# Input rows standardised on ScalarE with a scale and a bias, VectorE left with the bias column

## The reference, cut to what matters

```
def _layernorm(x, axis=-1, eps=1e-05):
    m = jnp.mean(x, axis=axis, keepdims=True)
    v = jnp.var(x, axis=axis, keepdims=True)
    return (x - m) / jnp.sqrt(v + eps)
...
    h = _layernorm(x, axis=-1) * (1 + ca) + sa
    x = x + ga * _L0_attn_ref(h, ...)       # q, k, v, gates; recurrent state; layernorm; silu gate; Wout
    h = _layernorm(x, axis=-1) * (1 + cb) + sb
    x = x + gb * _L0_ffn_ref(h, ...)        # router, top 2 of 8 experts, gelu
```

## Time and profile before

| | |
|---|---|
| median of 3 runs | 1010.74 us (1009.75 to 1011.5) |
| the profiled execution, its time | 1011.38 us |
| its span, first to last instruction | 1009.6 us |
| PE busy over the span | 902.7 us (89%) |
| DVE busy | 733.6 us (73%) |
| ACT busy | 479.1 us (47%) |
| POOL busy | 427.0 us (42%) |
| mean granted TensorE clock | 0.968 of full speed |

### The profile page before, as it was taken

One profiled execution on the slowest core, in us unless ns is written; L12 is line 12 of the kernel. 1 busy time (PEld: TensorE's weight loads), 2 busy tenths in 40 slices (PEclk: granted clock), 3 DMA queues, 4 the chain that ended last, 5 costly groups with the idle time before them and its releaser, 6 DMA issues.

```text
span 1009.6 us, 27138 instructions
## 1 busy us (share of the span) xinstructions
PE 902.7 (89%) x7313; PEld 743.9 (74%) x7314; DVE 733.6 (73%) x1909; ACT 479.1 (47%) x1548; POOL 427.0 (42%) x452
## 2 busy tenths in 40 slices
PE   4989999999999999997189999999999989999895
PEld 4556655656655656654179998999999989999895
DVE  2469999999999999997646666666566666666663
ACT  1556566666566665563034434343434433434432
POOL 5335665555655555653213333333323323233233
PEclk9789999999999999998579999999999999999998
DMA  7901111111111111111282222222222222222221
GB/s 240 375 27 52 54 45 51 53 39 52 53 42 53 53 38 53 53 38 39 83 278 40 39 37 37 38 43 32 43 32 43 39 36 38 37 38 38 39 39 24
DMA packets 51451, 62.68 MB, mean 62 GB/s; under 512 B 6273, under 2 KB 46930, under 8 KB 51282
## 3 DMA queue, kind: packets, MB, share of 16 engines
q1 hardware_dynamic: 38546, 44.36, 13.9%
q0 software_dynamic: 12864, 17.83, 10.3%
HBM read 38.91 MB, written 23.27 MB: 62 GB/s over the span
## 4 chain that ended last, share of the span: by engine, by line
PE 61%; DVE 14%; issue 9%; DVEq 6%; ACT 3%; SPq 3%; DMA 3%; POOL 0%; ACTq 0%; POOLq 0%
PE p_a L1084 19%; PE p_cum L1084 8%; PE p_z L1084 8%; PE p_qk L1084 8%; PE p_vg L1084 7%; PE p_o L1084 6%; DVE w_hi L842 4%; SPq L444 2%; PE p_tr L1084 1%; PE p_tr L1266 1%; DMA host_x<-in_L_attn_x_dram 1%; DVE x L917 1%; PE p_o L1103 1%; DVE host_s_r L1068 1%; DVEq L1033 1%
## 5 line engine op out<-in xcount | busy, mean ns | idle before, releaser
L641 POOL DMA_INDIRECT out_dram<-x,tok x68 | 163.6, 2405 | 344.3 <-DVE x L1061 318.7
L661 ACT ACTIVATE h2T<-p_tr,mods 128x128 f32<-128x128 f32 x200 | 80.6, 453 | 345.0 <-PE p_tr L1266 290.3
L1084 PE MATMUL p_a<-w_hi_r,host_s_r 128*128 x544 | 145.2, 299 | 11.8 <-DVE host_s_r L1068 11.8
L1084 PE MATMUL p_a<-w_r,host_s_r 128*128 x544 | 139.8, 289 | 0.0
L590 POOL TENSOR_TENSOR w<-qkT_both,own_half 128x512 f32<-128x512 f32 x64 | 65.0, 1035 | 165.4 <-ACT qkT_both L735 155.8
L1038 DVE COPY host_x<-w 128x1024 f32 x68 | 47.3, 696 | 98.0 <-issue 52.0
L1084 PEld LDWEIGHTS p_a<-w_hi_r,host_s_r 128*128 128x128 f32 x544 | 101.8, 187 | 14.2 <-issue 13.9
L1084 PEld LDWEIGHTS p_a<-w_r,host_s_r 128*128 128x128 f32 x544 | 101.9, 187 | 0.3
L842 DVE TENSOR_TENSOR w_hi<-p_a,upto 128x512 f32<-128x512 f32 x128 | 84.3, 679 | 4.1 <-PE p_a L1084 4.1
L621 POOL DMA_INDIRECT expert_rows<-rows,pos x64 | 63.9, 999 | 51.7 <-POOL rows L618 22.5
L1084 PE MATMUL p_qk<-h2T,host_x 128*128 128x128 f32 x544 | 68.8, 281 | 7.0 <-DVE qkT_both L1038 5.9
(11 more groups left out here) (208 smaller groups left out, 2085.4 us busy)
## 6 DMA issues: line engine op xcount, KB each, us to landing
w<-in_L_ffn_W_dram SPq DMA_DIRECT2D x16, 1024.0 KB, 12.5
ln_host<-expert_rows SPq DMA_DIRECT2D x68, 136.0 KB, 2.1
host_x<-in_L_attn_x_dram SPq DMA_DIRECT2D x64, 128.0 KB, 2.1
out_dram<-x SPq DMA_DIRECT2D x32, 128.0 KB, 1.7
w<-in_L_wmod_dram SPq DMA_DIRECT2D x1, 1536.0 KB, 6.4
expert_rows<-pad_rows SPq DMA_DIRECT2D x8, 136.0 KB, 1.8
out_dram<-x,tok POOLq DMA_INDIRECT x68, 4.7
b_all<-in_L_ffn_b_dram SPq DMA_DIRECT2D x1, 1024.0 KB, 7.5
```

What stands on the lines that cost most here:

```text
L641: nc.gpsimd.indirect_dma_start(out=out, out_offset=bass.IndirectOffsetOnAxis(ap=tok[u][:, 0:1], axis=0), in_=y_out[u][:], in_offset=None, ...
L661: last = A.activation(dst[:, j, :], src[:, j * P:(j + 1) * P], ACT.Identity, scale=mods[:, which + 2 + j:which + 3 + j], bias=mods[:, whic ...
L1084: return nc.tensor.matmul(dst, lhsT, rhs, start=start, stop=stop, skip_group_check=True)
```

## The change

DVE no longer writes the standardised rows. It waits for `x_scale` as before and makes one column, -mean * scale, in column 3 of `mv_x`, in one instruction of 128x1. ACT then writes `xn` as scale * x + bias in one `Identity` activation of 128x256, whose scale and bias are both columns of `mv_x`. A new semaphore `x_shift` goes from DVE to ACT. ACT does this between the gate's Ln (L714) and the copy of the output (L718). `xn_ready` now comes from ACT, and the wait for `xT_ready` of the chunk before, which guards `xn`, moves to ACT with it. For chunk 0 ACT does it right behind the inverse root.

```diff
+        x_shift = sem("x_shift")
...
+            def standardise_x(c, slot):
+
+                act_e.wait_ge(x_shift, c + 1)
+                after(act_e, xT_ready, c - 1)
+                A.activation(xn[slot][:], x_in[slot][:], ACT.Identity,
+                             scale=mv_x[:, 2:3], bias=mv_x[:, 3:4]).then_inc(xn_ready, 1)
+
             def modulate_x(c):
...
             inverse_root(mv_x, 0, x_stats, x_scale)
+            standardise_x(0, 0)
             act_e.wait_ge(mods_taken, 1)
...
                     A.activation(lg[:], eg[:], ACT.Ln, bias=1.0).then_inc(gate_log1p_ready, 1)
+                if nextx:
+                    standardise_x(s + 2, u)
                 if finish:
                     act_e.wait_ge(owT_ready, s)
...
             def norm_x_end(n, u):
-                after(dve, xT_ready, n - 1)
-                standardise(xn[u][:], x_in[u][:], mv_x, n, x_scale).then_inc(xn_ready, 1)
+                dve.wait_ge(x_scale, n + 1)
+                V.tensor_scalar(mv_x[:, 3:4], mv_x[:, 0:1], mv_x[:, 2:3], -1.0, ALU.mult, ALU.mult).then_inc(x_shift, 1)
```

## The result

The changed kernel takes 1025.35 us (median of 4 runs, 1024.51 to 1026.56), the kernel before 1011.12 us beside it: 14.2 us or 1.4% slower, ratio 1.014, 95% interval 1.0127 to 1.0153. Predicted were 1024.4 us, 13.7 more.

What follows compares the result with a forecast made beforehand. Bound: a dependence ring through PE, ACT and DVE, with ACT's and DVE's branches tied at L904. 13.5 us (steps 3 to 29) plus 0.2 (step 2) made 13.7, on 1010.74: 1024.4 us, range 1017 to 1028.

Steps and rivals of the forecast that it cites:

- The two tied branches: From L868, DVE's and ACT's parallel work meet at the forget gate L904; ACT's branch claimed as long, with nothing to spare.
- The ring: Loop of dependences x1, PE, ACT, DVE and back to x1; a delay of x1 goes round once every step.
- the other meeting on the ring: DVE's L942, claimed to be released by ACT's L748, starting 0.05 us after that ends.
- The price of the activation: Time the new Identity holds ACT between L714 and L718: 0.50 us per step, lower bound 0.31 to 0.33 us, upper 626 ns.
- 27 x 0.50: Cost over steps 3 to 29, which have the tight meeting at L904: 13.5 us.
- two estimates, 0.46 and 0.54: Two ways to price the activation's hold on ACT, in us: from L661, and from L714 plus the columns' cost.
- VectorE's relief: DVE ready 0.16 to 0.24 us earlier at `mask(2)`, taken as 0.2; worth nothing unless ACT's branch shortens too.
- the limit that the prediction had seen at 306.78: End of PE's scores, which `mask(2)` needs; `mask(2)` could start 0.2 us earlier than 306.98, at that time.
- the remark that VectorE's version gets its columns without a charge: Claim against the change: ACT pays for two column operands (92 ns for one in the trace), DVE does not.
- step 2: `mask(2)` still waits 0.59 us for PE there, hiding part of the insertion; cost 0 to 0.5 us, taken as 0.2.
- The faster one: Rival: ACT has 0.5 us of hidden slack ahead of L904, so DVE's relief gains 5.4 us, 1005.3 us; chance 0.07.
- PE's idle time ahead of `output_of_block(0)`: Sign in each step: PE's wait for the residual sum L917 grows from 0.92 to about 1.4 us.

Runs made afterwards that it cites:

- e5: Kernel before, with the Abs of both gates left out on ScalarE; 1011.26 us, ratio 1.0002.
- e3: Kernel before plus one extra ScalarE activation of the same form behind L714, reading constants that are loaded, writing an unread tile; VectorE still standardises; 1028.53 us.
- e8: Kernel before plus the same kind of extra, unread ScalarE activation behind L714, reading a tile GpSimd fills, so no new wait for loads; 1024.04 us.
- e1: Changed kernel, with the new activation stripped of its two column operands (scale 1, no bias); 1019.83 us, ratio 1.0083.
- e4: Changed kernel, with the Abs of both gates left out on ScalarE; 1005.46 us, ratio 0.9942.
- e7: Kernel before reordered so ScalarE and VectorE do the forget gate ahead of the gate, plus the change (ScalarE standardises); 1004.02 us, ratio 0.9924.
- e2: Changed kernel, with the new activation moved behind the forget gate's Ln (L725); 1015.88 us, ratio 1.0048.
- e9: Kernel before plus an extra, unread ScalarE activation behind the forget gate's Ln (L725); VectorE standardises; 1014.19 us, ratio 1.0027.
- e6: Kernel before reordered so ScalarE and VectorE do the forget gate ahead of the gate; VectorE standardises; 1001.35 us, ratio 0.9894.
- e10: Kernel before reordered with the forget gate ahead of the gate, VectorE standardising, and ScalarE's copy of q and k moved ahead of the gate; 1000.62 us.

## Why the prediction was right

*What bounds.* The two tied branches hold: e5 shows that VectorE's branch binds when ScalarE's is shortened, e3 and e8 that ScalarE's binds when it is lengthened. The ring holds as well, since each delay of the residual sum came again in the next step. That the profile charged no wait at L904 was no sign of slack. L942, the other meeting on the ring, is also closer than the prediction has it. It read L942 as released by ScalarE alone, but VectorE's own L936 ends at 311.99, 0.07 us after L942 starts, so there too both were as long.

*The price of the activation.* 0.49 us per step was measured, 0.50 taken; it lasts 585 ns. (That is the estimate that the prediction worked out from the Trainium skill, "ScalarE: Activation LUTs", section "What ACT_TABLE_LOAD costs"; the trace agrees.) e1 confirms that the columns are 0.19 us of it. The loop grew by 0.512 us per step, 13.8 us against 13.5. The step of the sum that is off is "27 x 0.50", by 0.3 us: in the odd steps the forget gate is later by 0.54 and not 0.49 us, with ScalarE's late Abs (see e8). The 0.50 was the middle of two estimates, 0.46 and 0.54; that it fell within 0.01 of the measured time is in part luck.

*VectorE's relief.* Taken as 0.2 us and worth nothing. It is 0.18 us in even steps (`mask(2)` at 3.37 instead of 3.55 us behind L868) and 0.25 in odd ones. In the even steps it could not be more, for `mask(2)` starts 0.03 us behind the end of PE's scores, the limit that the prediction had seen at 306.78. e4 shows its worth where ScalarE has cover: 0.17 and 0.26 us per step. The new column lasts 0.21 us, longer than the 0.16 that I put as its upper end, but the next instruction starts 0.13 us behind it. The column is part of that: L927, also 128x1 but without a column operand, lasts 0.13 us. So the remark that VectorE's version gets its columns without a charge is not borne out for an instruction this small; at 128x256 L792 and L917 both last 0.41 us, with columns and without, but they differ in more than that.

*The waits and step 2.* No wait at `x_shift` or for xn, 0.33 us at the product with Wout, hidden; step 2 cost 0.18 us, 0.2 were taken.

*The rivals.* The faster one needed 0.5 us of slack ahead of L904; there was none. But its worth, 5.4 us, is near what e4 found once the slack was made: 5.8 us. PE's idle time ahead of `output_of_block(0)` was foretold as 1.4 us; it is 1.22, and some of the rest stands ahead of the product with Wout, in every second step.

## What to carry to other kernels

Before work is moved to an engine with a low busy share, look up what that engine's queue has to deliver next, and compare the end of that with the start of the instruction that needs it. A start 0.05 us behind the producer's end meant here that there was no cover, even where the profile prints no wait, because the consumer's engine was busy until just then. An instruction moved onto a tied branch costs all the time for which it holds its engine (0.49 us here, of 585 ns), and the relief of the other branch is lost. The same move gained 5.8 us where the branch had cover and VectorE was still the limit (e4). It gained nothing where PE's scores had become the limit (e7). And a kernel in balance has more than one such place: after the first was cleared, the same engine bound at the next.

## What the hardware showed that I had not expected

Moving GpSimd's start by 0.4 to 0.5 us against VectorE changed VectorE's own lengths, by -0.2 us in one step and +0.45 in the next, 3 us in all (e2, e9). One instruction of 8 columns went from 0.24 to 0.65 us. In e7 a start at 0.86 us did the same to another, 0.97 us instead of 0.43. Starts at 0.05, 0.36, -0.35 and -0.9 us (before, e6, e5, e10) left the middle piece at 5.2 and 5.4 us. A theory of which meeting costs what would need runs of its own.

The kernel before has such meetings in every step. Behind the residual sum VectorE's L934, L935 and L936, of 1 and 8 columns, last 0.74, 0.78 and 0.65 us (medians of 26 steps), while GpSimd does the products of q and of the gate. Each of the 78 ends 0.01 to 0.03 us behind the end of an instruction of GpSimd. L928, a reciprocal of one column, lies inside an instruction of GpSimd and lasts 0.16 us, so not every instruction of VectorE is held. In e9, where GpSimd starts later, the first of the three lasts at most 0.25 us and the second 1.05 to 1.09.
